# Gathers of a graph layer issued five groups ahead of the products in place of eight

## What is computed

```python
deg_out = segment_sum(edge_weight, src, num_segments=N_NODES)
deg_in  = segment_sum(edge_weight, dst, num_segments=N_NODES)
norm = edge_weight * rsqrt(deg_out[src] * deg_in[dst] + EPS)

def _gcn_layer(x, W, b, src, dst, norm, n_nodes):
    xt = x @ W
    msg = xt[src] * norm[:, None]
    agg = segment_sum(msg, dst, num_segments=n_nodes)
    return relu(agg + b)
...
h6 = _gcn_layer(h5_all, W6, b6, src, dst, norm, N_NODES)      # layer 0
h7 = _gcn_layer(h6, W7, b7, src, dst, norm, N_NODES)          # layer 1
```

## Time and profile before

| | us |
|---|---|
| median of 3 runs | 5319.24 |
| lowest and highest run | 5316.11, 5332.93 |
| span of the profiled execution | 5305.9 |
| GpSimd busy in it | 2859.7 (54%) |
| TensorE busy | 3977.3 (75%) |
| VectorE busy | 2919.9 (55%) |
| GpSimd's gathers (L915), all four layers, 2504 | 2411.9 |

### The profile page before, as it was taken

One profiled execution on the slowest core, in us unless ns is written; L12 is line 12 of the kernel. 1 busy time (PEld: TensorE's weight loads), 2 busy tenths in 40 slices (PEclk: granted clock), 3 DMA queues, 4 the chain that ended last, 5 costly groups with the idle time before them and its releaser, 6 DMA issues.

```text
span 5305.9 us, 64097 instructions
## 1 busy us (share of the span) xinstructions
PE 3977.3 (75%) x20960; PEld 3151.6 (59%) x20961; DVE 2919.9 (55%) x7680; ACT 1417.2 (27%) x3894; POOL 2859.7 (54%) x3104
## 2 busy tenths in 40 slices
PE   6775655454555576777777996899996898886999
PEld 6653434343434455666666665787785777764666
DVE  7755655455546775555656556776665332243344
ACT  6603323232331222222222331333331000033221
POOL 7745566666656665565653002566565666643322
PEclk9857776777777777777777998999998999997999
DMA  3332343333333232222322002444444554444321
GB/s 92 106 70 78 110 112 100 98 99 99 97 95 90 86 87 79 81 85 81 86 81 66 25 14 74 130 144 144 138 146 140 160 155 138 138 136 135 103 80 54
DMA packets 337524, 535.23 MB, mean 101 GB/s; under 512 B 91587, under 2 KB 246452, under 8 KB 337186
## 3 DMA queue, kind: packets, MB, share of 16 engines
q0 software_dynamic: 133168, 361.15, 24.1%
q1 hardware_dynamic: 196902, 163.10, 10.0%
q10 hardware_dynamic: 7118, 6.83, 0.4%
HBM read 439.58 MB, written 94.26 MB: 101 GB/s over the span
## 4 chain that ended last, share of the span: by engine, by line
PE 54%; DVE 19%; issue 11%; another core or an unknown queue 11%; ACT 2%; DVEq 1%; POOL 1%; DMA 0%; ACTq 0%; SPq 0%; POOLq 0%
PE PSA L1091 15%; PE PSA L1239 12%; PE PSA L1486 4%; PE PSA L1472 4%; PE PSA L1248 4%; DVE ACC L2102 3%; PE PSA L1373 3%; PE PSA L1389 3%; DVE XIN L2075 2%; DVE XT L2075 2%; PE PSA L1041 1%; PE PSA L1219 1%; ACT ACC L1536 1%; DVE PSA L2066 1%
## 5 line engine op out<-in xcount | busy, mean ns | idle before, releaser
L915 POOL DMA_INDIRECT WORK<-tab,SRC x2504 | 2411.9, 963 | 1923.8 <-issue 666.6
L2102 DVE TENSOR_TENSOR ACC<-ACC,PSA 64x256 f32 x1296 | 541.9, 418 | 1221.2 <-remote 686.6
L1091 PE MATMUL PSA<-WORK,XIN 128*128 128x256 f32 x3032 | 881.2, 443 | 362.7 <-ACT XIN L1569 156.8
L1091 PEld LDWEIGHTS PSA<-WORK,XIN 128*128 128x128 f32 x3032 | 653.7, 225 | 490.5 <-issue 387.9
L1091 PE MATMUL PSA<-WORK,XT 128*128 128x256 f32 x1976 | 581.2, 446 | 217.8 <-ACT XT L1569 131.9
L1091 PEld LDWEIGHTS PSA<-WORK,XT 128*128 128x128 f32 x1976 | 427.7, 226 | 302.6 <-issue 226.4
L1239 PE MATMUL PSA<-WORK 128*128 128x256 bf16 x2730 | 367.0, 278 | 16.7 <-issue 16.5
L1239 PEld LDWEIGHTS PSA<-WORK 128*128 128x128 bf16 x2730 | 270.1, 100 | 60.7 <-issue 24.7
L2075 DVE TENSOR_TENSOR XIN<-PSA,DST 128x512 f32<-128x512 f32 x392 | 265.3, 679 | 3.9 <-issue 1.9
L1729 ACT ACTIVATE WORK<-PSA 128x512 bf16<-128x512 f32 x245 | 146.4, 598 | 428.1 <-PE PSA L1219 328.4
L1639 ACT ACTIVATE XIN<-XIN,HSB 128x128 f32<-128x128 f32 x504 | 160.2, 392 | 359.7 <-DVE XIN L2075 231.5
(11 more groups left out here) (511 smaller groups left out, 6768.4 us busy)
## 6 DMA issues: line engine op xcount, KB each, us to landing
WORK<-tab,SRC POOLq DMA_INDIRECT x2504
unit_counts_d<-WORK SPq DMA_DIRECT2D x245, 128.0 KB
WAX<-unit_counts_d SPq DMA_DIRECT2D x140, 128.0 KB
ACC<-in_L_ffn_w SPq DMA_DIRECT2D x16, 1024.0 KB
WORK<-unit_counts_d SPq DMA_DIRECT2D x105, 128.0 KB
tab<-WORK SPq DMA_DIRECT2D x98, 128.0 KB
slots_x<-FILL SPq DMA_DIRECT2D x4, 2080.0 KB
ACC<-slots_x SPq DMA_DIRECT2D x8, 910.0 KB
```

Source lines behind the costliest of these rows:

```text
L915: po.indirect_dma_start(out=rows[:, 0:width], out_offset=None, in_=tab[:, :], in_offset=bass.IndirectOffsetOnAxis(ap=SRC[:, c:c + 1].bitca ...
L1091: last = pe.matmul(PS[h][:, 0:D], chosen[:, j * P:(j + 1) * P], rows[:, 0:D], start=(j == 0), stop=(j == Q - 1))
L2102: return ve.tensor_tensor(rows, rows, PS[h][half, 0:D], ALU.add)
```

## The change

A constant `NEAR = 5` is added, and every group of layer 0 from the fifth on waits for the product five groups back, beside what it waited for already. Since five is less than 8 and 19, the new wait is the stricter one for each of these groups. It holds for groups 5 to 18 too, which had no wait for a product.

```diff
 AHEAD = 4
+NEAR = 5
 BEHIND = 5
@@ gather_edges
                     if layer == 0 and 2 <= g < ROUND:
                         po.wait_ge(s_dp, RS_ * (g - 1))
+                    if layer == 0 and g >= NEAR:
+                        po.wait_ge(s_p, g - NEAR + 1)
                     landed = (s_rx if in_x(layer, g) else s_row)[slot_of(layer, g)]
```

## The result

| | before | changed |
|---|---|---|
| median of 4 runs, us | 5317.67 | 5351.98 |
| lowest and highest run, us | 5311.84, 5332.93 | 5335.99, 5359.34 |
| span of the profiled execution, us | 5305.9 | 5357.7 |

The changed kernel is slower: the ratio is **1.0061**, 95% interval 1.0040 to 1.0081. On another chip, with 12 runs of the changed kernel, it was 1.0051 (1.0034 to 1.0068). The forecast was 5344 us, +0.46%.

What follows compares the result with a forecast made beforehand. GpSimd's gathers were taken to set layer 0's pace, 5.74 us a group. Degree phase -33, more groups at 5.77 us each +57, end 0: +24.4 on a 5305.9 span, plus 13.3 to the median, 5344 us; range 5275 to 5400.

Steps and rivals of the forecast that it cites:

- Term 1: Degree phase of layer 0: without gathers of groups 5 to 18 beside it, the first product comes 33 us earlier.
- Term 2: Layer 0's long stretch: 203 groups left after the first product instead of 189, the 31.95 us wait gone.
- Term 3: GpSimd's gathers at a lead of five: bursts of four groups, 5.77 us a group, bounds 5.01 and 6.06.
- product h+2: Second product after the last one seen at a burst's start; claimed to end at about T + 10.5 to 11.
- Term 4: From layer 0's last gather to layer 1's first, 25.10 us idle: no change, bounds -5 and +3.
- Shorter bursts that cost less: GpSimd's bursts in layer 0: shorter ones get signals back early; half the pauses gone gives 5264 us; chance 0.21.
- The lead as the bound: GpSimd's bursts in layer 0 end after three groups with pauses as long, about 6.02 us a group, 5398; chance 0.17.
- The degree phase that gives nothing: Degree phase: its blocks are held by something other than gathers, term 1 is 0, 5376 us; chance 0.09.
- The wait that does nothing: The added wait in layer 0 is idle and the time would be 5319 us; chance 0.02.

Runs made afterwards that it cites:

- degree_free: The kernel before, with only groups 5 to 18 made to wait for the first product, leads of 19 and then 8 kept; ratio 1.0095.
- drain3: The kernel before, with GpSimd from group 46 on also waiting after every third group until that group's own rows have landed; ratio 1.0035.
- steady5_one: The kernel before up to group 45; from group 46 on the product five back is the only wait; ratio 1.0002.

## Why the prediction was right, and where it was not

**Direction and size.** Slower was forecast by 0.46%, and 0.61% (0.40 to 0.81) was measured. The end of layer 0 was forecast at +24.4 us and came at +26.7, on the last chip at +29.3. On the last chip the four terms below come to -29.6 + 48.9 + 16.9 - 6.9 = 29.3. That the sum is this near is luck in part: its third term was too small and its fourth too large.

**Term 1, the degree phase** (-33): first gather after the degrees 385.83 against 419.71, **-33.9**; selection 96 is 34.6 earlier, and the blocks of 8 selections take 7.4 us each, as those without gathers did before. Right. On the last chip it was -29.6 (383.78 against 413.39). degree_free shows it alone: -33. The sum of the prediction has the stream start at 386.9, where 33 off 419.71 is 386.7; nothing hangs on this.

**Term 2, more groups in the stream** (+48.8 before any change of pace): with one wait, where the pace didn't change, 203 groups took 1155.6 us on the last chip against 1106.7 for 189, **+48.9**. Right.

**Term 3, the pace** (5.77, +8.4 us): the wrong step. I had product h+2 end too late to be seen, so bursts of four groups. In the trace products are let through in the middle of a burst (the additions at 614.70 and 619.17), and 26 of the bursts after group 46 have five groups, with pauses of 3.9 us in the mean. That alone would have cost nothing: five with one wait has 5.695 to 5.701. What did cost was a term that the sum did not have. The change adds a wait to groups that already had one, and I priced the value that is waited for, not the instruction: each restart is 0.4 to 0.5 us later, and the pace dearer by 0.10 us a group (5.795 against 5.695). Over 203 groups the stream is 1172.4 against 1155.6 us, **+16.9 where I had +8.4**. The restarts don't account for all of it: 35 to 42 of them after group 46 make some 12 of the 16 us there, an estimate from their number and their mean. That these 203 groups took 5.78 us each on the last chip, near my 5.77, is luck: the kernel before went at 5.69 there, not at the 5.64 and 5.74 that I started from.

**Term 4, the end** (0, bounds -5 to +3): 20.41 against 25.10, -4.7, and on the last chip 18.95 against 25.81, **-6.9**, beyond the bound. I had said "at most as many" held products and put their worth at nothing. In the profiles this time is 23.7 to 26.1 us at a lead of eight (six kernels, drain3 with its forced pauses apart), 18.9 to 21.1 at five (six) and 18.7 at four: it goes with the lead. That held products are the reason is not shown. This error and that of term 3 are of opposite sign and hide each other, which is why the total looks better than its parts.

**The rivals.** Shorter bursts that cost less: no, the bursts got longer, and a lead of four didn't shorten them below four groups. The lead as the bound: no at five; at four the pace is the same too, but there VectorE waits for rows, and whether the lead bounds that kernel is open. The degree phase that gives nothing: no. The wait that does nothing: no, though steady5_one shows that its value, from group 46 on, does nothing to the pace; its instruction does. Repeated gaps can mean too few buffers, says the Trainium skill ("Perfetto Trace Analysis", Optimization Strategy). These traces show no price of fewer buffers down to four groups in flight: gaps of 3.1 to 3.2 us at four, 3.2 after four and 3.8 after five groups at eight, and the same pace.

## What to carry to other kernels

Count waits as instructions: a second wait on an engine that restarts some 40 times, each time at the end of a pause that sets the pace, was over half of this loss (15.7 of 29.3 us in layer 0), and where a new wait includes the old one it should replace it. A transfer that is issued ahead is only worth what it is hidden behind: 14 groups beside the degrees cost 30 to 34 us there and save 49 in the stream, while the same 14 groups let go after them, in one unbroken run, were paid back as a wait of 32 us, 0.95% in all. And when the pace of a stream stays the same at three sizes of its buffer, look at what each engine waits for before you call the buffer harmless: at eight VectorE waited for products, at four for rows.

## What the runs showed of the hardware that I had not expected

- One wait more before a GpSimd gather, already satisfied by the same signal as its neighbour, moves the restart from 0.11 us behind the signal to 0.53 to 0.60 in the mean. Mid-burst it costs little: the rests stay at 0.30, but one or two times in groups 46 to 207 a rest of 1.67 stands behind the first gather of a group, which no kernel with one wait shows.
- With one wait per group, the pace of layer 0's gathers is 5.69 to 5.75 us at a lead of 4, 5 and 8, though the bursts are different: at a lead of four 4 groups with 3.15 us of pause; at five 5 groups with 3.7, 4 with 2.4 to 2.7 and single ones with 2.2; at eight 4 and 5 groups with 3.2 and 3.9. At eight the pause grows by 0.7 us with the fifth group; that 4 groups have 2.4 at a lead of five shows that the length of the burst alone doesn't set it. A forced silence of mostly 2.1 us after three groups wasn't enough to free what the products wait for and gained nothing.
- While gathers flow without a pause, products get through for a while and then rarely. In degree_free five additions start in the first 28 us and two in the next 42, with VectorE waiting up to 19.27 us; in the changed kernel one gets through 18 us into a burst. TensorE's handshakes with ScalarE ahead of the first product were not delayed by the same gathers.
- Why signals of products are seen late while GpSimd issues gathers stays open. No run changed the size or the number of rows of a gather.
